# Attention with 16 heads: the causal mask of the weights' scores by a GpSimd select after the exponential instead of a TensorE matmul before it

## The reference, cut to what matters

```python
q = jax.nn.silu(x @ Wq.T)
k = jax.nn.silu(x @ Wk.T)
v = jax.nn.silu(x @ Wv.T)
...
scores = jnp.einsum('bhnd,bhmd->bhnm', q_dir, k_dir)
...
mask = jnp.tril(jnp.ones((N, N), dtype=bool))
scores = jnp.where(mask, scores, -jnp.inf)
probs = jax.nn.softmax(scores, axis=-1)
out = jnp.einsum('bhnm,bhmd->bhnd', probs, v)
out = out.transpose(0, 2, 1, 3).reshape(B, N, D)
return out @ Wo.T
```

## Time and profile before

| | us |
|---|---|
| three runs | 4521.71, 4528.04, 4534.21 |
| median | 4528.04 |
| profiled execution | 4522.78 |
| its span | 4520.9 |

### The profile page before, as it was taken

The page is one execution under the profiler, slowest core; times in us unless marked ns, Lnnn a source line. Parts: engine busy times, 40 slices in busy tenths (PEclk is TensorE's granted clock), DMA queues, the critical chain, the costliest instruction groups (busy, mean ns, idle before and its releaser), DMA issues. The chain is left out here.

```text
span 4520.9 us, 70654 instructions
## 1 busy us (share of the span) xinstructions
PE 3809.7 (84%) x26056; PEld 2647.9 (59%) x26088; DVE 2532.4 (56%) x4540; ACT 1895.9 (42%) x3440; POOL 2013.8 (45%) x2061
## 2 busy tenths in 40 slices
PE   7677787799999439948998799788888888999995
PEld 3546664467676239924554455466666666656663
DVE  6667453455554662247777322598888887412223
ACT  4132133333333102226666322588888886112222
POOL 6312462222223126632332111399999998332223
PEclk9788898899999769978999899899999999999997
DMA  5747541200000629945554200111111111822224
GB/s 192 242 144 218 150 117 64 75 10 10 13 17 8 222 74 296 288 122 150 150 145 135 84 29 28 51 52 50 52 50 44 49 45 58 273 89 46 46 45 133
DMA packets 334072, 459.67 MB, mean 102 GB/s; under 512 B 71222, under 2 KB 245750, under 8 KB 329606
## 3 DMA queue, kind: packets, MB, share of 16 engines
q1 hardware_dynamic: 311094, 424.27, 30.7%
q0 software_dynamic: 22512, 30.36, 3.6%
q10 hardware_dynamic: 128, 0.52, 0.0%
HBM read 314.54 MB, written 140.51 MB: 101 GB/s over the span
## 5 line engine op out<-in xcount | busy, mean ns | idle before, releaser
L3565 POOL TENSOR_TENSOR mamba_hC<-mamba_h_t,mamba_cb 128x512 f32<-128x512 f32 x512 | 677.7, 1351 | 70.4 <-DVE mamba_h_t L3078 64.5
L3078 DVE TENSOR_TENSOR_SCAN mamba_h_t<-mamba_dA,mamba_pB 128x512 f32<-128x512 f32 x512 | 596.8, 1206 | 122.1 <-PE mamba_pB L3456 46.0
L3456 PE MATMUL mamba_pB<-ident,mamba_dBT 128*128 128x128 f32 x2048 | 328.6, 285 | 55.4 <-DVE mamba_h_t L3078 49.5
L3254 ACT ACTIVATE mamba_dA<-mamba_delta,mamba_a_neg 128x512 f32<-128x512 f32 x512 | 356.7, 713 | 23.5 <-DVE mamba_h_t L3078 22.9
L3456 PEld LDWEIGHTS mamba_pB<-ident,mamba_dBT 128*128 128x128 f32 x2048 | 239.8, 144 | 191.9 <-issue 100.2
L3465 PE MATMUL mamba_pY<-ident,mamba_hC 128*128 128x128 f32 x2048 | 320.3, 280 | 15.8 <-POOL mamba_hC L3565 14.2
L1911 POOL TENSOR_SCALAR mqa_prob<-mqa_prob,mqa_rinv 128x128 f32<-128x128 f32 (+3 forms) x256 | 136.2, 532 | 425.4 <-DVE mqa_rinv L1687 424.4
L2350 DVE TENSOR_REDUCE mha_nmax<-mha_pM 128x1 f32<-128x384 f32 (+3 forms) x352 | 215.5, 634 | 104.0 <-PE mha_pM L2658 100.8
L3245 ACT ACTIVATE mamba_dBT<-mamba_eT,mamba_b_t 128x512 f32<-128x512 f32 x384 | 273.7, 713 | 0.1
L1501 POOL DMA_INDIRECT top_sum<-top_y,top_xg x71 | 110.3, 1554 | 352.1 <-ACT top_y L1290 341.5
L3465 PEld LDWEIGHTS mamba_pY<-ident,mamba_hC 128*128 128x128 f32 x2048 | 247.3, 145 | 25.2 <-POOL mamba_hC L3565 24.4
(11 more groups left out here) (618 smaller groups left out, 8877.8 us busy)
## 6 DMA issues: line engine op xcount, KB each, us to landing
expert_w<-in_L_ffn_W SPq DMA_DIRECT2D x48, 1024.0 KB, 5.9
delta_shared<-delta_w SPq DMA_DIRECT2D x64, 576.0 KB, 4.9
mamba_cb<-mamba_c SPq DMA_DIRECT2D x128, 256.0 KB, 3.2
mha_qkT<-mha_parts_d SPq DMA_DIRECT2D x96, 256.0 KB, 4.9
expert_w<-in_L_ffn_W SPq DMA_DIRECT2D x48, 256.0 KB, 6.4
top_w<-in_L_ffn_w SPq DMA_DIRECT2D x24, 512.0 KB, 10.6
delta_w<-delta_wst SPq DMA_DIRECT2D x17, 576.0 KB, 3.4
top_slots<-top_y SPq DMA_DIRECT2D x1, 9159.0 KB, 36.9
```

The lines of the kernel that those rows point to most:

```text
L3078: nc.vector.tensor_tensor_scan(h_t[:, n % RH, :], dA[:, n % RA, :], pB[n % 2][:, :], 0.0, ALU.mult, ALU.add).then_inc(z["scan_ready"], 1)
L3254: nc.scalar.activation(dA[:, n % RA, :], delta[:, a % 2, ct, :], ACT.Exp, scale=a_neg[:, ct, s:s + 1])\
L3456: last = nc.tensor.transpose(pB[n % 2][:, tok(t)], dBT[:, r % RS, t, ct * P:(ct + 1) * P], c.ident[:, :])
L3565: nc.gpsimd.tensor_tensor(hC[:, n % RO, :], h_t[:, n % RH, :], cb[:, r % RC, :], ALU.mult)\
```

## The change

TensorE no longer adds the mask to the weights' scores. After the exponential GpSimd selects on the 128x128 blocks on the diagonal: it keeps a weight where the query is not ahead of the key and writes 0 elsewhere. The weighing waits for the selects instead of the exponentials, and comes three ticks behind instead of two; with HOLD the turn of the maxima (TURN) and ScalarE's copy of the output bank come one tick later too. Four entries of GpSimd's table move.

```diff
-    HOLD = 2
+    HOLD = 3
     TURN = NU - 1 - LEAD + HOLD
...
-    POOL_AT = dict(rstd=-91, square=(-76, -75, -75, -68), scaled=(-56, -53, -50, -49), divide=(65, 66, 71, 73), scale=90, sum=97, spread=-129, whole=-108)
+    POOL_AT = dict(rstd=-91, square=(-72, -71, -70, -68), scaled=(-50, -50, -49, -49), divide=(65, 66, 71, 73), scale=90, sum=97, spread=-119, whole=-108)
...
                     for i in range(m):
-                        nc.tensor.matmul(out[:, i, :], qkT[:, b % 2, 1, h + i, k * P:(k + 1) * P], qkT[:, b % 2, 0, h + i, k * P:],
-                                         start=(i == 0), stop=False, skip_group_check=True)
-                        last = nc.tensor.matmul(out[:, i, 0:P], c.ident16[:, :], c.causal16T[:, :],
-                                                start=False, stop=True, skip_group_check=True)
+                        last = nc.tensor.matmul(out[:, i, :], qkT[:, b % 2, 1, h + i, k * P:(k + 1) * P],
+                                                qkT[:, b % 2, 0, h + i, k * P:], start=(i == 0), stop=(i == m - 1),
+                                                skip_group_check=True)
...
-                    pe.wait_ge(exp_ready, mine[-1] + 1)
+                    pe.wait_ge(causal_ready, mine[-1] + 1)
...
+                def drop_later_keys(unit):
+                    k, _, m = weight_units[unit % NU]
+                    pool.wait_ge(exp_ready, unit + 1)
+                    diagonal = by_unit(prob[:, unit % BUF, :], m, L - k * P)[:, :, 0:P]
+                    nc.gpsimd.affine_select(out=diagonal, in_=diagonal, compare_op=ALU.is_ge, fill=0.0, base=0,
+                                            pattern=[[0, m], [1, P]], channel_multiplier=-1).then_inc(causal_ready, 1)
...
                 for t in TICKS:
+                    if 0 <= t - 1 < ALL:
+                        drop_later_keys(t - 1)
                     if due(t, POOL_AT["spread"]):
```

More of the change, by code:

```diff
@@ L2072, in stage_silu_mha @@
          v_ready, len_ready, len_st, len_in, fac_ready, fac_st, fac_in, scaled, high_ready, rest_ready, mid_ready,
-         low_ready, h_st, m_st, l_st, slots_in, a_ps, max_ready, nm_ready, nmT_ps, nmT_ready, s_ps, exp_ready, o_ps,
+         low_ready, h_st, m_st, l_st, slots_in, a_ps, max_ready, nm_ready, nmT_ps, nmT_ready, s_ps, exp_ready, causal_ready, o_ps,
          oS_ready, sums_st, sums_in, rinv_ready, rinv_st, rinv_in, oT_ready, xr_in, y_var, y_scale, yn_ready, y_out,
@@ L2079, in stage_silu_mha @@
                 "fac_in", "scaled", "high_ready", "rest_ready", "mid_ready", "low_ready", "h_st", "m_st", "l_st",
-                "slots_in", "a_ps", "max_ready", "nm_ready", "nmT_ps", "nmT_ready", "s_ps", "exp_ready", "o_ps",
+                "slots_in", "a_ps", "max_ready", "nm_ready", "nmT_ps", "nmT_ready", "s_ps", "exp_ready", "causal_ready", "o_ps",
                 "oS_ready", "sums_st", "sums_in", "rinv_ready", "rinv_st", "rinv_in", "oT_ready", "xr_in", "y_var",
```

## The result

The changed kernel takes 4568.73 us in the median of 6 runs (4563.03 to 4572.82), the kernel before 4527.39 in 6 runs beside it (4521.71 to 4540.38). The ratio is 1.0078, with a 95% interval of 1.0062 to 1.0094: 35 us slower, between 28 and 43; the two medians lie 41 us apart. That is in the predicted range and 15 us above the predicted 4554. The direction was right. As the experiments show, the sum was not made of the right parts, so that it comes this near is in part luck.

A forecast was written before the change was run, and what follows sets the result against it. TensorE's instruction order bounds about 45 of 66 us of a batch, a chain around it the other 20. New waits of 47.5 us less 21 from the masks add 26.5 to 4528.04: 4554, range 4518 to 4580.

The forecast's parts named there:

- rival 4: Masks not on the path, the maxima's two banks hold TensorE: nothing gained, 40 us lost, 4568; 50% together with the forecast.
- Gain of the masks: Part 1, TensorE's 512 mask matmuls at 0.055 us: 21 us gained, between 14 and 28.
- Waits for selects: Part 2, TensorE's weighing waits behind GpSimd's ordered work: 47.5 us of new waits, (a) to (g) together.
- (a): Tick 2, output norm's scales hold up selects before tile 0's weighing: 2.2 us in batches 2 to 7, 13.2 us.
- (f): Batch 6, selects wait behind divisions whose DMA lands late: TensorE late by 7.9 us.
- (d): Tick 41, the input norm's scale delays two selects: 0.8 us in batches 2 to 5, 3.2 us.
- (e): Factor chain, one select between GpSimd's second and third product: 0.3 us in six batches, 1.8 us.
- (b): Tick 9, residual's sum ahead of a select: 1.5 us in batches 2 to 4, less in 5 and 7, 5.8 us.
- (c): Ticks 17 to 22, squares and divisions between selects: 1.6 us at tick 21, 0.9 at tick 24, 12.3 us total.
- rival 2: Every loop is real but overlaps the one before: 24 us of waits against 21, 4531; 20%.
- Rival 3: GpSimd and VectorE block each other at shared SBUF ports, and the clock may fall: 4574; 13%.
- (g): Batches 6 and 7, short ticks without projections, divisions and selects run late: 1.8 and 1.5 us, together 3.3.

The follow-up runs named there:

- e2_masks: The kernel before without the 512 mask matmuls, nothing in their place: ratio 0.9961, 18 us faster.
- e1_tables: The kernel before with HOLD = 3 (weighing, transposition, output copy a tick later) and GpSimd's changed table; masks stay, no selects: ratio 1.0057, 26 us slower.
- e3_no_select: The changed kernel without its selects, weighing waits for the exponentials: ratio 1.0053 to the kernel before, 24 us slower.
- e9_later_weigh: The kernel before with weighing and output copy a tick later (HOLD = 3), transposition at its old ticks: ratio 1.0030, 14 us slower.
- e10_no_select_turn: The changed kernel without its selects and with the transposition at its old ticks: ratio 1.0020 to the kernel before, 9 us slower.
- e7_pool_ticks: The kernel before with only GpSimd's changed table of ticks: ratio 1.0001, 0 us.
- e5_turn: The changed kernel with the transposition of the maxima back at its old ticks: ratio 1.0074 to the kernel before, 34 us slower.
- e8_turn_sum: e5_turn with the residual's sum at tick 14 instead of 9: ratio 1.0060 to the kernel before, 27 us slower.
- e4_spare: The changed kernel with its selects going to a buffer nobody reads, TensorE not waiting for them: ratio 1.0042 to the kernel before, 19 us slower.
- e11_hold4: e8_turn_sum with the weighing another tick later (HOLD = 4): ratio 1.0033 to the kernel before, 15 us slower.
- e12_late_divide: e11_hold4 with the four divisions at ticks 30 to 33 instead of 21, 22, 27 and 29: ratio 1.0000 to the kernel before, 0 us.

## Why the prediction came out as it did

The range and the sign were right, and the cause named, GpSimd's order, is real; but by the middle value it is a third of the loss as the change was made, not all of it. That 4569 came within 15 us of 4554 is luck: waits for selects that were put at about twice their worth or more stand against 27 us of shifts that were put at 0 and masks that gave back almost nothing. That it is within 1 us of rival 4's 4568 is luck too, since rival 4 adds 40 us of waits for selects.

- **Gain of the masks, 21 us.** Right by itself: 18 us (e2_masks), 35 ns a mask (22 to 46) where the prediction took 55 on 380 of 512. The Trainium skill ("TensorE: Matmul & The Clock Gate", Back-to-back issue gap) has about 81 ns as the spacing of such a stream; the measured gain is further below it than the starts were. What failed is that it was added: beside the later weighing the masks gave 2 and 5 us, give or take 11 and 8 (e1_tables to e3_no_select, e9_later_weigh to e10_no_select_turn). The matmuls' wait for maxima is longer without the masks in both pairs, 28.6 to 34.5 and 32.9 to 43.8 us. Rival 4's cause was wrong for the kernel before and nearly right for the kernel after. A batch was to be 2.3 us shorter without masks; the first seven of e2_masks are 2.4 in the mean.
- **HOLD and TURN, taken as 0.** This is the step that failed. "The transposition of the maxima moves one tick later and keeps three ticks to its user", put at 0, asked who needs the result, not what the instruction and its neighbours covered. The transposition costs 13 us by itself, the later weighing 14 (taken as 0, at most 7 of gain). The prediction named VectorE's maxima only in rival 4, as a limit on the gain, not as what becomes bare when TensorE's order shifts.
- **GpSimd's table, 0 apart from meetings with selects.** Right (e7_pool_ticks).
- **Waits for selects, 47.5 us.** The mechanism was right, the size was not: they are worth 25 us with the old transposition, 11 with the late one. (a) and (f) are there: 1.22 us in each of six batches, 6.87 us in batch 6 (7.9 predicted). For (a), 2.2 us were predicted; 1.22 for the select and 0.77 just before for a maximum make 2.0, but the 0.77 belong to the later weighing. (d) is 0.58 us in each of four batches (0.8 predicted). Of (e) the two pairs of products are there; the select between them lasts 0.74 us, for 0.3 predicted. (b) and (c) show only with the old transposition, in e5_turn with 1.53 us in three batches and 0.94 a time (1.5 and 1.6 predicted); in the change TensorE has already lost that time to VectorE (1.81 us at tick 10, 0.66 at tick 19). The prediction took TensorE's old times as its times in every batch, and waits in a row as a sum; rival 2, "every loop is real but overlaps the one before", describes it best.
- **The tests of the sum, "40 us or more" and "wrong if less than 20".** The first is met only if the rows of weight loads and matmuls are added, 24.0 + 18.2, and 11 us of that are the same time twice: 31 together, so it is not met. The second turns on the row: 18.2 us on the matmuls is under 20, 24.0 on the weight loads is over. What the prediction drew from it, that GpSimd's order then does not reach TensorE and the time is 4515, is refuted either way: each wait of (a), and that of (f), is ended by a select.
- **Rival 3, the port and the clock.** At most some 7 us at the sum and the low parts, by e8_turn_sum, which does not part them from the selects behind the sum; e4_spare shows that the selects' own meetings with VectorE cost nothing that can be measured. The granted clock was 0.81 from 2484 to 2510, most of it ahead of the long wait, which began at 2506.7, so this fall is not the wait's doing. In e11_hold4 it fell in the wait, as the rival had it. Over the whole stage it was 0.98 before and 0.97 in the changed kernel.
- **Select prices.** 0.292, 0.415 and 0.661 us were predicted. The groups of the changed kernel by form (count; busy us, mean ns of one; idle before):

```profile
L2760 POOL TENSOR_SCALAR_AFFINE_SELECT mha_prob<-mha_prob 128x128 f32<-128x128 f32 x256 | 83.0, 331 | 173.1 <-ACT mha_prob L2492 172.0
...
L2760 POOL TENSOR_SCALAR_AFFINE_SELECT mha_prob<-mha_prob 128x256 f32<-128x256 f32 x64 | 29.0, 461 | 27.7 <-ACT mha_prob L2492 27.5
...
L2760 POOL TENSOR_SCALAR_AFFINE_SELECT mha_prob<-mha_prob 128x512 f32<-128x512 f32 x32 | 20.3, 635 | 3.6 <-ACT mha_prob L2492 3.3
```

Most last what was predicted (the median of all 352 is 292 ns); the means are longer for one and two heads by some that last up to 0.87 us, like the two beside VectorE's low part above.

What stays open: how far the masks' lost gain and the select waits depend on single batches; the parts do not add (-18 + 14 + 13 + 0 + 25 = 34 happens to come near 35, but in pairs they overlap by 10 to 15 us), and no run undid (b), (d) or (g) alone. Nor were the sum at tick 14 and the late divisions tried on the kernel before, whose low parts last 812 ns in the mean; they might make it faster as well, so e12_late_divide's tie with it does not say that selects are as good as masks.

## What to carry to other kernels

In a kernel that runs by a hand-written order, an instruction is also the cover of whatever another engine does beside it. Before a step is moved by a place, look at which waits of TensorE are short only because that step stands there, above all in a ring of two banks; moving it and taking work off it should be priced together, since the work taken off shows as time only where no other wait takes its place. And when a wait is added behind an engine's queue, give it slack first at the places where that queue waits for a DMA.

## What the runs showed of the hardware

The low part (L2327), a VectorE operation with two inputs in SBUF, lasted until the GpSimd operation beside it was over and most of its own time on top. The one from 2273.64 ended at 2275.92, 0.56 us behind the sum, which ended at 2275.36; the median of the low parts is 0.68 us. The Trainium skill ("SBUF — State Buffer", SBUF: two separate sides) has a pair of ports shared by the two engines as an exclusive lock for the whole instruction; the trace agrees. It goes the other way as well: two selects of two heads took 1.45 us together behind that sum (row at 2275.32 above), of which the first 0.60 lie beside that low part; the select just ahead of the sum took 0.41.
